# A recurrent stack on one core: the middle layer's batch stage reworked, and GpSimd's sums cut into eight pieces

## The reference

```
x = x + rnn(x)            # h = tanh(x_t Wx + b + h Wh)            one step per position
x = x + ssm(x)            # conv = conv_b + sum_k x_{t+k-3} * cond[k];  proj = conv @ Wp + bp
                          # B = softplus(proj[:64]); C = tanh(proj[64:]); u = x @ Ws + bs
                          # state = decay * state + dt * B * u;  y = (C * state) @ Wo + bo
x = x + lstm(x)           # four gates of 512, one step per position
x = x + x @ (base + A B)  # a low-rank layer made from cond
```

## Time and profile before

| | |
|---|---|
| median of 3 runs | 4427.27 us (4425.87 to 4428.75) |
| the profiled execution's own time | 4419.02 us |
| its span | 4417.1 us |
| TensorE / VectorE busy | 3655.3 us / 3634.3 us |
| ScalarE / GpSimd busy | 1559.4 us / 1291.6 us |
| mean granted TensorE clock | 0.983 |

### The profile page before, as it was taken

The page is one execution under the profiler, slowest core; times in us unless marked ns, Lnnn a source line. Parts: engine busy times, 40 slices in busy tenths (PEclk is TensorE's granted clock), DMA queues, the critical chain, the costliest instruction groups (busy, mean ns, idle before and its releaser), DMA issues.

```text
span 4417.1 us, 252254 instructions
## 1 busy us (share of the span) xinstructions
PE 3655.3 (83%) x106672; PEld 2960.4 (67%) x106672; DVE 3634.3 (82%) x20882; ACT 1559.4 (35%) x6724; POOL 1291.6 (29%) x4519
## 2 busy tenths in 40 slices
PE   7888888888888888888888888888888888888775
PEld 4566667676667676666676666777666767666653
DVE  5588888888888888888888888888888888888766
ACT  4233333333333333333333333333333333333321
POOL 0223332233332223333233333232333222333311
PEclk9899999999999999999999999999999999999999
DMA  7100000000000000000000000000000000000000
GB/s 247 42 4 9 9 6 8 8 6 8 8 6 8 8 6 8 8 8 6 8 9 6 8 8 6 9 8 6 8 8 6 9 8 6 8 6 4 6 5 7
DMA packets 18979, 62.51 MB, mean 14 GB/s; under 512 B 3942, under 2 KB 4510, under 8 KB 14834
## 3 DMA queue, kind: packets, MB, share of 16 engines
q1 hardware_dynamic: 17612, 46.54, 3.3%
q10 hardware_dynamic: 294, 0.33, 0.0%
HBM read 38.34 MB, written 8.39 MB: 11 GB/s over the span
## 4 chain that ended last, share of the span: by engine, by line
DVE 40%; PE 33%; ACT 11%; POOL 8%; issue 7%; SPq 1%; DMA 1%; DVEq 0%; ACTq 0%; POOLq 0%
PE ps_lstm L968 30%; DVE lstm_sums L754 11%; DVE lstm_arg L760 7%; DVE lstm_h_scaled L783 4%; ACT lstm_gates_2c L521 4%; ACT lstm_tanh_c L526 3%; DVE lstm_gates_2c L771 3%; POOL stage L371 3%; DVE lstm_ig_fc L766 2%; DVE lstm_h_parts L791 2%; POOL stage L372 2%; DVE rnn_h_parts L857 2%; DVE lstm_h_parts L787 2%; DVE lstm_o_scaled L775 2%; DVE rnn_arg L821 2%
## 5 line engine op out<-in xcount | busy, mean ns | idle before, releaser
L968 PE MATMUL ps_lstm<-lstm_Wh_parts,lstm_h_parts 128*20 128x256 f16 x65472 | 2027.8, 276 | 638.1 <-DVE lstm_h_parts L791 633.2
L968 PEld LDWEIGHTS ps_lstm<-lstm_Wh_parts,lstm_h_parts 128*20 128x20 f16 x65472 | 1508.0, 92 | 1146.6 <-DVE lstm_h_parts L791 945.3
L521 ACT ACTIVATE lstm_gates_2c<-lstm_arg 128x32 f32<-128x32 f32 x2048 | 469.8, 229 | 1624.7 <-DVE lstm_arg L760 1623.8
L754 DVE STREAM_TRANSPOSE lstm_sums<-ps_lstm 128x256 f32<-128x256 f32 x2048 | 912.1, 445 | 137.1 <-PE ps_lstm L968 86.9
L344 POOL COPY lstm_sums<-lstm_in 128x32 f32<-128x32 f32 x2048 | 417.8, 213 | 1368.2 <-DVE lstm_arg L760 1354.5
L1007 PE MATMUL ps_rnn<-rnn_Wh_parts,rnn_h_parts 128*20 128x128 f16 x32736 | 646.7, 221 | 46.2 <-DVE rnn_h_parts L859 46.1
L760 DVE TENSOR_REDUCE lstm_arg<-lstm_sums 128x32 f32<-128x96 f32 x2048 | 536.0, 262 | 120.9 <-DVE lstm_sums L754 19.6
L1007 PEld LDWEIGHTS ps_rnn<-rnn_Wh_parts,rnn_h_parts 128*20 128x20 f16 x32736 | 550.9, 93 | 99.1 <-DVE rnn_h_parts L859 82.7
L526 ACT ACTIVATE lstm_tanh_c<-lstm_gates_2c 128x8 f32<-128x8 f32 x2048 | 413.2, 202 | 394.3 <-DVE lstm_gates_2c L771 384.4
L546 ACT ACTIVATE rnn_h<-rnn_arg 128x16 f32<-128x16 f32 x1024 | 221.2, 216 | 771.0 <-DVE rnn_arg L821 771.0
L857 DVE TENSOR_SCALAR rnn_h_parts<-rnn_h 128x16 f16<-128x16 f32 x1024 | 240.0, 234 | 292.1 <-ACT rnn_h L546 292.1
(11 more groups left out here) (176 smaller groups left out, 3390.3 us busy)
## 6 DMA issues: line engine op xcount, KB each, us to landing
layer_plus_2I<-in_L_cond_w SPq DMA_DIRECT2D x16, 1024.0 KB, 6.1
out<-out_rows SPq DMA_DIRECT2D x128, 64.0 KB, 1.9
x_rows<-in_x SPq DMA_DIRECT2D x31, 256.0 KB
lstm_Wx<-in_L_cond_Wh SPq DMA_DIRECT2D x1, 4096.0 KB, 19.2
lstm_Wx<-in_L_cond_Wx SPq DMA_DIRECT2D x1, 4096.0 KB, 14.2
layer_plus_2I<-in_L_cond_Wh SPq DMA_DIRECT2D x1, 1024.0 KB, 9.3
rnn_Wx<-in_L_cond_Wx SPq DMA_DIRECT2D x1, 1024.0 KB, 11.3
lstm_in<-in_L_cond_w SPq DMA_DIRECT2D x1, 1024.0 KB, 9.1
```

Source lines behind the costliest of these rows:

```text
L521: A.activation(gate[h][:, 0:G, :].rearrange("p g q -> p (g q)"), arg[h][:, :, :].rearrange("p g n -> p (g n)"), ACT.Tanh, scale=gate_scale ...
L754: return mark(V.transpose(tr[h][s % 2][:, :, 0:QC], psL[h][:, 0:HW].rearrange("p (g c) -> p g c", c=QC)))
L968: ins = mm(psL[h][QC * j:QC * j + LO + NB, 0:HW], hls[:, k, :], whl[:, k, h, e, j, :], start=(k == 0 and e == 0), stop=(k == KB - 1 and e ...
```

## The change

The batch stage of the middle layer is done in another way, and other batch work moves to other steps:

- The convolution is folded into Wp: once, in chunk 0, ScalarE scales Wp by the taps (`wpk`, 16 instructions), and B and C become 16 products each of x1 at four offsets. All mid tensors lie on 128 partitions: sequences 0 and 1 on the lower 64, 2 and 3 on the upper 64, 64 values each. TensorE makes u, B and C as 36 pairs of products (`tile_position` (0,0) and (0,64)), weights 64 columns wide, 64 moving columns, in steps 0 to 3 (8, 12, 12 and 4 pairs). GpSimd and ScalarE have no convolution any more.
- The softplus is VectorE's: 17 instructions of 128x64 (or 32 of them) from step 3 to step 8, with a polynomial of six terms; part 0 stands where it stood, part 2 between the rnn's reduction and the wait for its tanh.
- Wo is laid out twice with zeros (`wo2`), so the products with it are 8 of 64 columns (step 9); x1 is added by TensorE, one product with the identity in each of steps 5 to 8. GpSimd's L436 is gone.
- XT_STEP 0 becomes 3, L0_STEP 7 becomes 5, L2_STEP 14 becomes 12, OUT_STEPS become 4, 10, 11, 28, HOLD_STEPS 29 to 31; copies out of PSUM follow one step behind their products, one a step.
- PIECES becomes eight pieces of four positions. In step z GpSimd does x1's piece, in step z+1 x3's, each behind a wait for half 0's products of that step.
- In the prologue Wp, Ws and Wo are loaded ahead of the lstm's 4 MB of weights, and the low-rank layer is built in the even steps of chunk 1 in one PSUM bank.

```diff
-PIECES = [(0, 14), (14, 24), (24, 30), (30, 32)]
+PIECES = [(a, a + 4) for a in range(0, CT, 4)]
-XT_STEP = 0
-OUT_STEPS = [1, 2, 6, 13]
-HOLD_STEPS = [11, 30, 31]
-L0_STEP = 7
-WO_STEP = 12
-L2_STEP = 14
+XT_STEP = 3
+OUT_STEPS = [4, 10, 11, 28]
+SSM_MMS = [("u", TAPS - 1, b) for b in range(KB)] + [(c, k, b) for c in "BC" for k in range(TAPS) for b in range(KB)]
+SSM_CUTS = [0, 8, 20, 32, 36]
+EXP_STEP = 2
+SERIES_STEP = 3
+CT_STEP = 5
+L0_STEP = 5
+X1_STEP = 5
+WO_STEP = 9
+X2_STEP = 10
+HOLD_STEPS = [29, 30, 31]
+L2_STEP = 12
...
 # gpsimd
                     for a, z in PIECES:
-                        if s == z:
-                            residuals(a, z)
+                        if w["rnn"] and s == z:
+                            if w["lstm"]:
+                                pool.wait_ge(S["lstm_mm0"], s + 1)
+                            x1_piece(a, z)
+                        if w["lstm"] and s == z + 1:
+                            pool.wait_ge(S["lstm_mm0"], s + 1)
+                            x3_piece(a, z)
...
 # vector, ssm_stage(s, part)
+                    if s == SERIES_STEP and part == 0:
+                        vec.wait_ge(S["exp_ready"], 1)
+                        m_den[0] = mark(V.tensor_scalar(den, ez, 2.0, None, ALU.add))
+                    if s == SERIES_STEP and part == 2:
+                        vec.wait_ge(S["vec_done"], m_den[0])
+                        mark(V.reciprocal(rden[:, 0:HT], den[:, 0:HT]))
+                    if s == SERIES_STEP + 1 and part == 0:
+                        m_den[0] = mark(V.reciprocal(rden[:, HT:HS], den[:, HT:HS]))
...
+                    if s == SERIES_STEP + 2 and part == 2:
+                        series(pol_b, pol_a, LOG1P[4], qr)
+                        series(pol_a, pol_b, LOG1P[3], qr)
...
+                    if s == SERIES_STEP + 4 and part == 2:
+                        vec.wait_ge(S["vec_done"], m_p[0])
+                        at = mark(V.scalar_tensor_tensor(out=drive, in0=psS[:, HS:2 * HS], scalar=b_u, in1=bt, op0=ALU.add, op1=ALU.mult))
+                        vec.wait_ge(S["vec_done"], at)
+                        scan(0)
...
 # vector, the step
                         reduce_rnn(s, r_at)
+                    if w["mid"]:
+                        ssm_stage(s, 2)
+                    if w["rnn"]:
                         vec.wait_ge(S["rnn_tanh"], s + 1)
...
 # tensor
+                    if w["mid"] and s < len(SSM_CUTS) - 1:
+                        if s == 0:
+                            pe.wait_ge(S_last["x1_ready"], len(PIECES))
...
+                        for q in range(SSM_CUTS[s], SSM_CUTS[s + 1]):
+                            c, k, b = SSM_MMS[q]
+                            w_ = dict(u=ws[:, b, :], B=wpk[:, k, b, 0:NS], C=wpk[:, k, b, NS:2 * NS])[c]
...
+                            for h in range(2):
...
+                                last = mm(o_.rearrange("p (t n) -> p t n", n=2), w_, x1T[1 - par][:, b, k:k + CT, 2 * h:2 * h + 2],
+                                          start=first, stop=end, tile_position=(0, NS * h))
...
+                    if w["mid"] and X1_STEP <= s < X1_STEP + KB:
+                        b = s - X1_STEP
+                        mm(psX[:, TOK * b:TOK * (b + 1)], ident[:, :], x1T[1 - par][:, b, HALO:HALO + CT, :].rearrange("p t n -> p (t n)"),
+                           start=(b == 0), stop=False)
...
                         for b in range(KB):
-                            w_ = wo[:, P * b:P * (b + 1)]
-                            last = mm(psX[:, TOK * b:TOK * (b + 1)], w_, y[:, :], start=True, stop=True)
+                            x2_ = psX[:, TOK * b:TOK * (b + 1)].rearrange("p (t n) -> p t n", n=NB)
+                            for h in range(2):
+                                last = mm(x2_[:, :, 2 * h:2 * h + 2], wo2[:, h, P * b:P * (b + 1)], y3,
+                                          start=False, stop=(b == KB - 1 and h == 1))
```

More of the change, by code:

```diff
@@ L175, in resid_stack_kernel @@
         tc = [sb(f"lstm_tanh_c{h}", [P, HB * NB]) for h in range(NH)]
[L177 to L185, removed]
+        zabs, zmax, ez, den, rden, sr, qr, bt, ct, drive, y, pol_a, pol_b, st_ = [
+            stage[:, 3 * 512 + HS * q:3 * 512 + HS * (q + 1)] for q in range(14)]
+        wpk = stage[:, 6 * 512:10 * 512].rearrange("p (k b c) -> p k b c", k=TAPS, b=KB)
+        wo2 = stage[:, 10 * 512:12 * 512].rearrange("p (h d) -> p h d", h=2)
+        states = st_.rearrange("p (t n) -> p t n", n=2)
+        st0 = sb("state0", [P, 2])
+        spw = sb("softplus_work", [P, 9, 2])
         whl32 = wxl
@@ L358, in fill_rnn, with x1_piece, x3_piece @@
                     Q.tensor_copy(tr_r[s % 2][:, :, XS:XS + NB], xr[par][:, :, s, :]).then_inc(S["rnn_x_filled"], 1)
[L360 to L385, removed]
+                def x1_piece(a, z, par=par, S=S):
+                    pool.wait_ge(S["rnn_tanh"], z)
+                    Q.tensor_tensor(x1T[par][:, :, HALO + a:HALO + z, :], xT[par][:, :, a:z, :], hr[:, :, a:z, :], ALU.add
+                                    ).then_inc(S["x1_ready"], 1)
+                def x3_piece(a, z, par=par, S=S):
+                    for h in range(NH):
+                        pool.wait_ge(S[f"lstm_h_ready{h}"], z)
+                    Q.tensor_tensor(x3s[par][:, :, a:z, :], x2s[par][:, :, a:z, :], hl[:, :, a:z, :], ALU.add
+                                    ).then_inc(S["x3_ready"], 1)
                 if w["lstm"]:
@@ L438, in body @@
[L438 removed]
+                    if w["rnn"] and w["mid"] and s == HALO_STEP:
                         pool.wait_ge(S_last["x1_ready"], len(PIECES))
@@ new lines, in ssm_stage @@
+                    if s == SERIES_STEP + 5 and part == 0:
+                        m_p[0] = scan(1)
+                    if s == SERIES_STEP + 5 and part == 2:
+                        vec.wait_ge(S["vec_done"], m_p[0])
+                        vec.wait_ge(S["ct_ready"], 1)
+                        mark(V.tensor_copy(st0[:, :], states[:, CT - 1, :]))
+                        V.scalar_tensor_tensor(out=y, in0=st_, scalar=spt[:, 1:2], in1=ct, op0=ALU.mult, op1=ALU.mult
+                                               ).then_inc(S["y_ready"], 1)
@@ L936, in prepare @@
                     last.then_inc(w2_mm, 1)
+                if r == CB_STEP:
+                    pe.wait_ge(d_ssm, 16 * 4)
+                    for c in range(2):
+                        for b in range(KB):
+                            for h in range(2):
+                                last = mm(psL0[NS * h:NS * (h + 1), c:c + 1], wp[:, b, NS * c:NS * (c + 1)], b_conv[:, b:b + 1],
+                                          start=(b == 0), stop=(b == KB - 1), tile_position=(0, NS * h))
+                    last.then_inc(cb_mm, 1)
                 if r in H0_STEPS:
                     k = H0_STEPS.index(r)
+                    if k == 0:
+                        pe.wait_ge(cb_ready, 1)
                     pe.wait_ge(l_src, G * (k + 1))
```

372 lines of the change are left out of this document (174 added, 198 removed).

## The result

The changed kernel takes 4198.95 us (median of 4 runs, 4189.99 to 4205.91) against 4428.01 for the kernel before (4425.87 to 4432.25): a ratio of 0.948, with a 95% interval of 0.946 to 0.95.

The account below looks back on a forecast made before the run. No engine was full; the middle layer's batch stage caused most of 9.9 us lost a chunk. Removed 9.2, added 5.3: 3.9 x 31 = 121 us, prologue 4, so 4419 became 4294, plus 8 for the median: 4302 (4235 to 4410).

Parts of the forecast that it names:

- TensorE, steps 0 to 3: Middle layer's paired products on TensorE at 0.058 us a record, beyond 1.50 us free a step: 3.35 us added a chunk.
- rival 4: Loads of two column groups run side by side, so steps 0 to 3 cost nearly nothing: 4198 us; 7%.
- 128 x 0.111: Upper bound for steps 0 to 3, load and stream one after the other at 0.111 us a record: 9.2 us.
- rival 1: Middle products run serially on TensorE in steps 0 to 3, 9.2 us instead of 3.35: 4483 us; 8%.
- Wo in step 9: Wo's 16 records of 128 columns on TensorE take 1.78 us, 0.28 over the free time (0 to 0.8).
- the softplus series on VectorE: VectorE's 17 instructions in steps 3 to 8, mostly hidden in slacks: 1.0 us a chunk (0 to 4.3).
- the pieces: GpSimd's 14 sums of 0.32 us briefly hold VectorE, 0.05 us each: 0.7 us a chunk (0 to 2.8).
- Removed, 9.2 of 9.9: Of 9.9 us lost a chunk, the middle layer's batch stage (8.8) and step 24's old piece (0.4) go.
- Rival 2: VectorE's softplus instructions and GpSimd's sums aren't hidden and meet around L857: 3.3 us more a chunk, 4404 us; 15%.
- Rival 3: GpSimd's waits really hold its sums, which then run beside transpositions: 0.7 us less a chunk, 4280 us; 7%.
- The store's go: SyncE's go comes near 1.5 us into step 31, TensorE needs it near 2.1: costs nothing.
- Prologue: Earlier Wp, Ws and Wo copies cost 3 us, spreading chunk 1's low-rank products saves 7: net -4 us.

Follow-up runs that it names:

- c_hold2: The changed kernel with both of GpSimd's waits ahead of its pieces moved to half 0's products of the next step; 4190.27 us, ratio 0.9469.
- e_wo64: The changed kernel with each of Wo's products cut into two of 64 columns in alternating column groups; 4174.58 us, ratio 0.9436.
- h_best: The changed kernel with the edits of e_wo64 and c_hold2 together; 4161.12 us, ratio 0.9409.
- b_nohold: The changed kernel without the two waits for half 0's products ahead of GpSimd's pieces; 4196.8 us, ratio 0.9484.

## Why the prediction missed

**The step that failed** is "TensorE, steps 0 to 3": "I take the load's 0.058 a record", which lets the loads of both column groups follow each other at the pace of one. The forecast put 3.35 us a chunk there. Measured, steps 0 to 3 are 3.88, 3.81, 3.88 and 4.08 in the mean, 0.45 above four quiet ones. The difference, 2.9 us x 31 = 90, is nearly the whole miss of 4294 - 4201 = 93 for the profiled execution; what else was off, below, nearly cancels in it. The bound below it ("the pace of the lstm's four groups, 0.03") was in the text and was what happened, 0.030; I gave it 7% as rival 4. The trace of before had the nearest evidence for it in the earlier trace rows, where four column groups side by side make 0.03 a record (fp16 loads of 20 columns, though), and none that loads of different groups hold each other up; the 0.058 was worked out from loads that followed each other in one group or filled all columns. A pace measured within one group was carried over to two.

The sum beside it has a slip as well: "128 x 0.111" leaves out u's 16 records, for 36 pairs are 144 records, the number behind the 3.35. The upper bound is 144 x 0.111 + 1.0 - 6.0 = 11.0 and not 9.2, rival 1 would take some 4540 and not 4483, and it decides above 0.085 a record and not 0.095. None of it changes the forecast.

Loads overlapped here with running products of the same rows: the 48 loads of a step are busy for 1.49 us of the 1.63 us that their 48 products take. By the Trainium skill, "TensorE: Matmul & The Clock Gate", part 3, a load overlaps with products in flight only when the row group differs; here the row group is the same in all 48 records. The trace disagrees with it.

**Point by point**, excess over 32 quiet steps a chunk, forecast and measured (124.58 - 121.6 = 2.98):

| | forecast | measured |
|---|---|---|
| steps 0 to 3, TensorE | 3.35 | 0.45 |
| Wo in step 9 | 0.28 | 0.33 |
| the softplus series on VectorE | 1.0 with scans | 0.2 for twelve of its instructions |
| steps 4 to 8 and 10 to 30, all else in them | 0.7 for the pieces | 1.2 (1.41 less the 0.2) |
| step 31, the loop's end | in the 0.7 left of 9.9 - 9.2 | 0.79 |

- *Removed, 9.2 of 9.9*: right as far as it can be told; the stage's loss, set at 8.8, is 8.72 in the mean of steps 0 to 13. GpSimd is off the chain, most chunks have no stretch at half the clock, and no engine waits for the polynomial. What remains beside TensorE's and Wo's terms is 2.2, where the forecast had 2.4.
- *VectorE's series*: twelve of its instructions cost 0.2 where they stood for 0.9, too dear by 0.7. Rival 2 is out.
- *The pieces*: the wait is void, x1's piece starts at 3.42 of the step, L873 is held by 0.12: right. Rival 3's version is worth nothing a chunk alone (c_hold2) and 0.29 a chunk, 9 us, on top of e_wo64 (h_best), where 0.7 and 22 us were named; from step 10 on the time was given back anyway.
- *The store's go*: costs nothing, right; moving it changed nothing.
- *The loop's end*: not seen. 0.3 us a chunk more than before, though the store was not its cause.
- *Prologue*: the first lstm transposition is at 199.4 instead of 203.4, the forecast's -4. b_nohold and c_hold2, with the same prologue, have it at 197.3 and 201.6, so the exact figure is luck.
- *The end*: the last lstm chunk lasts 127.4 instead of 121.7, at a mean granted clock of 0.906 instead of 0.972; 5.7 us that the forecast didn't have. In two stretches of 20 us in it TensorE is busy for 10.9 and 13.1 us, since the batch work has ended, and the granted clock is 0.83 and 0.74. The median of the runs lay 8 us above the profiled execution before, and 2 below it after: 10 us that no step could give.

The chances: 63% for a number whose main term had bounds from 0 to 9.2 (rightly 11.0) and no row of the right kind between them was too much. What lay nearest in kind (alternating column groups, 0.03) should have had at least the weight of what lay nearest in weight size.

## What to carry to other kernels

Read a pace of TensorE with the place of its neighbours: products in different column groups ran side by side (0.030 us a record with 64 columns), products in one group one behind the other (0.056 with 64, 0.115 with 128), so cutting a product in two across column groups can halve its time, and the order in which two groups are issued was worth 96 us of 4295 here. Work that is put into an engine's slack costs what is left after the give-back, here 0.2 us a chunk where 0.9 was forecast. Whether removing a delay gains anything depends on what stands behind it: from step 10 on it gained nothing, in steps 4 to 8 0.32 us, and that showed in the time only once the overrun of step 9 and the stall at the jump were gone. A part of a change tried alone can lose by meeting work that the whole change removes. Compare the step at a loop's jump by itself: it can move by 0.8 us for an edit elsewhere in the program.

## What the runs showed of the hardware that I had not expected

- Two column groups need not strictly alternate: in the order two and two, where no two neighbours load the same weights, 48 records took 1.70 us against 1.63 in turns and 2.84 apart. Whether the load or the stream sets the 0.056 within one group isn't told apart by these runs, since both have 64 columns.
- TensorE's idle time at the loop's jump was 2.14 us in the chunk shown, put down to "issue", with an unchanged step body around it; eight idle products a chunk brought the odd chunks' last step from 5.27 to 4.54.
- VectorE and GpSimd: an instruction of 0.17 us took 0.29 when a piece of 0.32 had begun 0.07 ahead of it, while a transposition of 0.45 out of PSUM that had begun 0.05 ahead of such a piece kept its 0.45, and the piece its 0.32.
